# A small matmul group and its vector follow-up moved within a batch, and a scatter bound given as a number

## The reference

```
x = _layernorm(x + attn_block(x))
x = _layernorm(x + expert_block(x))
```

```
aff = x @ centroids.T
assign = jnp.argmax(aff, axis=1)
order = jnp.argsort(assign)
...
h = _layernorm(xs, ln_g[e], ln_b[e])
h = jax.nn.relu(h @ w1[e].T + b1[e])
ye = xs + h @ w2[e].T + b2[e]
...
out_sorted = alpha * y + (1.0 - alpha) * xs
```

## Time and profile before

| | |
|---|---|
| median of 3 runs | 836.34 us (836.01 to 836.52) |
| profiled execution, own time | 836.34 us |
| its span, first to last instruction | 834.6 us |
| TensorE matmul busy | 816.1 us, 98% |
| VectorE busy | 527.5 us, 63% |
| ScalarE busy | 347.7 us, 42% |
| GpSimd busy | 281.5 us, 34% |
| mean granted TensorE clock | 0.995 of full speed |

### The profile page before, as it was taken

The page is one execution under the profiler, slowest core; times in us unless marked ns, Lnnn a source line. Parts: engine busy times, 40 slices in busy tenths (PEclk is TensorE's granted clock), DMA queues, the critical chain, the costliest instruction groups (busy, mean ns, idle before and its releaser), DMA issues.

```text
span 834.6 us, 19341 instructions
## 1 busy us (share of the span) xinstructions
PE 816.1 (98%) x7250; PEld 544.0 (65%) x7250; DVE 527.5 (63%) x1526; ACT 347.7 (42%) x579; POOL 281.5 (34%) x392
## 2 busy tenths in 40 slices
PE   8999999999999999999999999999999999999994
PEld 5546476466567557547647646869999967776673
DVE  5475367757757867776877775524688555565652
ACT  1443414523531540641451352333332466577660
POOL 3503110512503313233142161325465454433522
PEclk9999999999999999999999999999999999999997
DMA  6710300040030030031021034224643897978930
GB/s 254 210 57 7 91 7 1 29 101 0 27 103 1 5 76 1 1 87 43 1 63 41 1 95 140 111 91 133 217 171 120 319 325 253 345 290 304 346 138 16
DMA packets 63939, 96.44 MB, mean 116 GB/s; under 512 B 39332, under 2 KB 52261, under 8 KB 55911
## 3 DMA queue, kind: packets, MB, share of 16 engines
q1 hardware_dynamic: 58550, 83.56, 30.0%
q0 software_dynamic: 4864, 11.10, 4.3%
q10 hardware_dynamic: 432, 0.54, 0.2%
HBM read 84.22 MB, written 11.23 MB: 114 GB/s over the span
## 4 chain that ended last, share of the span: by engine, by line
PE 71%; DVE 16%; issue 5%; ACT 4%; POOL 2%; DMA 1%; DVEq 0%; POOLq 0%; ACTq 0%
PE ps L638 11%; PE ps L740 10%; PE ps L758 10%; PE ps L632 7%; PE ps L571 6%; PE ps L595 6%; PE ps L804 4%; PE ps L780 4%; DVE w_sb L1112 3%; PE ps L603 3%; PE ps L465 3%; DVE x3x L1112 3%; ACT arena L1620 2%; DVE st_ln L929 2%; DVE arena L1042 2%
## 5 line engine op out<-in xcount | busy, mean ns | idle before, releaser
L638 PE MATMUL ps<-ff2T,hT 128*128 128x256 f32 x512 | 121.6, 385 | 0.2 <-ACT hT L1612 0.2
L632 PE MATMUL ps<-x3x,ff1T 128*128 128x512 f32 x256 | 118.2, 605 | 0.1
L1620 ACT ACTIVATE arena<-ps 128x1536 f32<-128x1536 f32 (+3 forms) x49 | 65.1, 1329 | 113.2 <-DVE arena L1042 113.2
L638 PEld LDWEIGHTS ps<-ff2T,hT 128*128 128x128 f32 x512 | 94.3, 190 | 21.0 <-issue 8.1
L758 PE MATMUL ps<-w_sb,arena 128*128 x400 | 95.7, 382 | 0.0
L1836 POOL TENSOR_TENSOR rs_ln<-mv_ln,eps 128x4 f32<-128x4 f32 x24 | 5.2, 216 | 263.1 <-DVE mv_ln L936 263.1
L632 PEld LDWEIGHTS ps<-x3x,ff1T 128*128 128x128 f32 x256 | 46.0, 189 | 59.0 <-issue 50.7
L758 PEld LDWEIGHTS ps<-w_sb,arena 128*128 128x128 f32 x400 | 72.2, 190 | 16.0 <-issue 8.2
L571 PE MATMUL ps<-arena 32*128 32x512 f32 (+7 forms) x896 | 73.0, 434 | 3.1 <-ACT hT L1061 1.4
L1042 DVE SCALAR_TENSOR_TENSOR arena<-ps,arena 128x512 f32<-128x512 f32 (+4 forms) x59 | 45.1, 771 | 47.4 <-PE ps L595 27.8
L571 PEld LDWEIGHTS ps<-arena 32*128 32x128 f32 x896 | 36.0, 184 | 37.3 <-issue 17.6
(11 more groups left out here) (239 smaller groups left out, 1563.6 us busy)
## 6 DMA issues: line engine op xcount, KB each, us to landing
arena<-in_w SPq DMA_DIRECT2D x27, 1024.0 KB, 7.1
hT<-in_w SPq DMA_DIRECT2D x16, 1024.0 KB
wts<-in_w SPq DMA_DIRECT2D x9, 1024.0 KB, 5.6
w_sb<-in_w SPq DMA_DIRECT2D x8, 1024.0 KB, 6.5
token_store<-x SPq DMA_DIRECT2D x8, 520.0 KB, 3.9
arena<-in_x SPq DMA_DIRECT2D x8, 512.0 KB, 3.9
w_sb<-in_x SPq DMA_DIRECT2D x48, 64.0 KB, 2.6
arena<-in_epack SPq DMA_DIRECT2D x18, 134.0 KB, 3.6
```

The lines of the kernel that those rows point to most:

```text
L632: last = eng.matmul(ps[:, 6 + m % 2, :], ff1T[:, kd, m * P:(m + 1) * P], xT3[:, kd, :], start=kd == 0, stop=kd == KD - 1)
L638: last = eng.matmul(quarter(6, t), hT[:, m, t * P:(t + 1) * P], ff2T[:, m, :], start=m == 0, stop=m == FM - 1)
L1620: eng.activation(o, i, ACT.Relu).then_inc(s_sa, 1)
```

## The change

On TensorE the affinity moves from step 5, after the two weighings and before unit 5, to the end of step 4, after unit 4 and before scores piece 5. Its result goes to bank 7 in place of bank 6. Its own condition is now that unit 3 has been evicted (before: unit 4). The wait that keeps the next writer of its bank from overwriting it (`s_afd`) moves from unit 6 to unit 5. On VectorE `dve_affinity` moves, within step 5, from after the two `dve_turn_out` to ahead of them, right behind the mask of piece 5. The rank stays in bank 6 and in its place. On GpSimd the bound of the scatter is given as a number instead of a register.

```diff
@@ pe_ffn1
-            if 0 < b < NB - 1 and m == 6:
+            if 0 < b < NB - 1 and m == 5:
                 eng.wait_ge(s_afd, b)
@@ pe_affinity
             if g < NB - 2:
                 eng.wait_ge(s_x4t, g + 1)
-                eng.wait_ge(s_f1e, FM * (g + 1) + 5)
+                eng.wait_ge(s_f1e, FM * (g + 1) + 4)
@@ pe_batch
                 if b > 1 and n < len(VALUES):
                     pe_values(eng, b, 4, VALUES[n])
-                if n == 5 and g >= 0:
-                    pe_affinity(eng, g, 6)
                 for k in (UNITS1 if b == 1 else UNITS)[n]:
                     pe_unit(eng, f, k)
+                if n == 4 and g >= 0:
+                    pe_affinity(eng, g, 7)
                 if n == 5 and g >= 0:
                     pe_rank(eng, g, 6)
@@ dve_batch
+                if n == 5 and g >= 0:
+                    dve_affinity(eng, g, 7)
                 if n == 3 and b == 0:
                     dve_ln2(eng, 1)
                 if n == 5:
                     dve_turn_out(eng, b, 0)
                     dve_turn_out(eng, b, 1)
-                if n == 5 and g >= 0:
-                    dve_affinity(eng, g, 6)
@@ slot_pool_scatter
-        def slot_pool_scatter(eng, j, most):
+        def slot_pool_scatter(eng, j):
...
-                                   in_=oo[u], in_offset=None, bounds_check=most,
+                                   in_=oo[u], in_offset=None, bounds_check=N_TOK - 1,
@@ pool_program
-            most = eng.to_reg(N_TOK - 1)
...
-                slot_pool_scatter(eng, j - 2, most)
+                slot_pool_scatter(eng, j - 2)
```

## The result

The changed kernel takes 841.0 us (median of 6 runs, 840.82 to 841.27) against 836.39 (6 runs) before. That is 4.6 us slower; 3.4 were forecast. The ratio is 1.0057, with a 95% interval of 1.0046 to 1.0067, or 3.8 to 5.6 us.

What follows compares the result with a forecast made beforehand. TensorE was taken to bound every batch: +1.13 us for piece 5's later start less 0.57 for the affinity's old place, +0.56 in six batches, 3.4 on 836.34, so 839.7 us. Range 839.1 to 840.9, widened to 838.2 to 841.2.

Steps and rivals of the forecast that it cites:

- the sum: Six batches: +1.13 us for piece 5's later start, -0.57 for the affinity's removal, +0.56 net each, 3.4 in all.
- part 5: Scatter bound as a number on GpSimd: -0.07 to +0.04 us at the last scatter, taken as 0.
- What bounds the kernel: TensorE bounds every batch, with 0.21 us visible idle per batch; only its idle time can hide new work.
- the delay is made good later: Rival: TensorE's idle time in batches and tile part swallows at most 1.6 us, leaving +1.8, 838.1 us; chance 6%.
- Part 1: Affinity taken out of step 5: 0.57 us off the path per batch, no wait removed with it.
- Part 2: Affinity between unit 4 and piece 5: held by unit 3's eviction, so piece 5 comes 1.13 us later.
- The allowance of -0.1 to +0.2 per batch: Room for one switch less or two more between kinds of matmul on TensorE: 2.8 to 4.6 us in all.
- Part 3: New wait ahead of unit 5 on TensorE: turned affinity ready with 0.67 us of margin, no cost.
- unit 5 waits: Rival: turned affinity late, TensorE stalls again; 0.3 us beyond the margin gives 5.2 us, 841.5; chance 4%.
- Part 4: VectorE's affinity operations, 1.4 us, ahead of the two turn-outs: cost nothing, covered by VectorE's idle time.
- the rival at -1.9 us: Neither bank 7 nor token turning holds the affinity; it fills the 0.31 us hole, 834.5 us; faster than 0.2%: 5%.
- the clock falls: Rival: TensorE's stops drop its clock to 1.2 GHz from piece 5 to the rank, 50 us, some 886; chance 1%.

Runs made afterwards that it cites:

- e8_move_turn4: Kernel before plus the affinity's move alone (bound in a register), with one token transpose shifted behind mask 4: 837.74 us against 836.29 before.
- e3_evict_first: Kernel before plus the affinity's move alone, with ScalarE evicting unit 3 ahead of relu 4 in batches 2 to 7: 840.16 us against 841.08 before.
- e4_wait_order: Kernel before plus the affinity's move alone, with the affinity's two waits swapped, eviction first, then turned tokens: 844.39 us against 841.08 before.
- e5_behind_scores: Kernel before plus the affinity's move alone, but placed directly behind scores piece 5, still in bank 7: 836.31 us against 836.29 before.
- e1_number_only: Kernel before with only the bound of all 34 scatters given as a number: 841.96 us against 841.08 before.
- e7_number_last: Kernel before with the bound given as a number in the last of the 34 scatters only: 837.17 us against 836.29 before.
- The two single parts: Kernel before with the affinity's move alone (bound in a register), +3.6 us, and kernel before with the bound as a number alone, +0.9 us.

## Why the prediction was right, and where its sizes were off

- **Where it landed.** 841.0 us lies in the range of 838.2 to 841.2, but 0.1 above the range that the sum itself gave (839.1 to 840.9). The wider range was meant for a delay partly made good and for a stall of unit 5, and neither came. So the direction and the main cause were forecast, and that the number fell inside is partly luck: a cost priced at nothing (0.9 us, part 5) was caught by room left for other things.
- **What bounds the kernel.** Right: 0.67 us per batch on TensorE came through six batches undiminished. The rival "the delay is made good later" is out: from the affinity that follows batch 7 to the end of the kernel the traces of the kernel before and of e8_move_turn4 take 280.5 us each, though e8_move_turn4 comes to that point 1.4 us later, which is 6 x 0.23.
- **Part 1, nothing is returned but the affinity's own 0.57.** Right. Piece 5 to rank took 8.35 us before and takes 7.78.
- **Part 2, the gate is the eviction of unit 3.** Right, shown by e3_evict_first and e8_move_turn4. The size was off: piece 5 was to come 1.13 us later and comes 1.24 later (hole and affinity 1.55 against the hole of 0.31). The missing 0.10 is the start of the affinity 0.14 behind the eviction; I had taken the 0.04 that a single wait showed in the earlier trace rows. e4_wait_order shows in its trace that it goes with the separate semaphore instruction. Six times 0.10 is 0.6 of the 1.2 us missed. The allowance of -0.1 to +0.2 per batch covered it, for a wrong reason: it was meant for switches.
- **Part 3, unit 5's wait is free.** Right, with the 0.67 us of margin; e5_behind_scores confirms it. The rival "unit 5 waits" is out.
- **Part 4, VectorE's order is free.** Right, by the same run.
- **Part 5, the bound as a number, -0.07 to +0.04 us.** Wrong. It costs 0.9 us at the last scatter (e1_number_only, e7_number_last; 0.94 in the traces). I priced the move by its duration, 35 ns, and the DMA by the difference in durations in the earlier trace rows. Both durations did stay: 29 ns and 1036 ns. What changed is the distance between wait and start, which no row of durations holds. The forecast asked what the added instruction takes and not which instruction carries the wait afterwards.
- **The sum.** By the traces 6 x 0.67 = 4.0 for the batches and 0.94 for the last scatter, 4.9 in all; measured 4.6, with 4.9 inside its interval. The two single parts measured 3.6 and 0.9.
- **The hole of 0.31.** It was no input to the sum, but to the rival at -1.9 us: a hole between two starts contains the 0.09 of the switch, so 0.21 is all that can be won per batch, -1.3 us.
- **A slip in a rival.** The 886 us of "the clock falls" are 836.3 + 50; with the forecast's own 3.4 they would be 890. Nothing hangs on it.
- **The clock.** The granted clock stayed at 1.00, the upper level, through holes of 0.81 us behind the modelled end in each of six batches, as it had through the 1.06 us of the earlier trace rows, which is measured the same way. The swing between the two levels of which the Trainium skill tells, in the section "A second HAM failure mode: psum-queue depth-cycling" of "TensorE: Matmul & The Clock Gate", is in no batch of any trace here.

## What to carry to other kernels

When a piece of work is moved into a hole, find what ends each of its own waits and compare with the hole's end, not its start; an engine that works off a list may hold back an event long after the data are there, and swapping two entries of that list (e3_evict_first) can be worth more than the move. Price an added instruction by who carries the wait once it is there: 29 ns of register move cost 0.9 us at the end of the chain. To shorten a chain that ends in a hole, look for work that can step behind its first link: one transpose, moved so in each of six batches, was worth 1.3 us.

## What the runs showed of the hardware

- The scatter, an indirect DMA on GpSimd, mostly starts 0.29 us behind the event it waits for when it carries the wait itself, and 0.81 us behind when a register move ahead of it does. For the last scatter the figures are 1.08 and 2.02.
- On TensorE, a start behind a wait that has an instruction of its own came 0.14 us after the event, against 0.04.
- Switching from units (128 x 128) to scores (32 x 128) with nothing to wait for takes 0.09 us of TensorE. It goes with the tile shape: in batch 0 of the kernel before, a group of 128 x 128 ends at 25.58 as modelled and the next of the same shape starts at 25.42, 0.16 earlier; that one ends at 29.02 and the next, of 128 x 64, starts at 28.95, only 0.07 earlier.
- Chips differ for this kernel: 841.08 against 836.29 us for the same code. On the slower one all four kernels traced, with the affinity in its old place and in the new one, have a stop in batch 7's step 5 that ends on nothing the profile names. The timeline of PE in e1_number_only:

```profile
497.24 2.03 PE L595 MATMUL ps<-arena 64*32 64x192 f32 x41
499.44 0.65 PE L595 MATMUL ps<-arena 64*32 64x256 f32 x5 [0.17 <-issue]
500.88 0.60 PE L595 MATMUL ps<-arena 64*32 64x256 f32 x2 [0.79 <-issue]
```

The profiled execution of the changed kernel has the same stop (2.0 us) and the same smaller ones later, so its 845.33 us are more likely such a chip's than the change's. What stops TensorE there was not tested and stays open.
